# A vision block on one core: output projections in half-precision parts, second scores in full precision, a bank for each use

## The reference

```
tokens: patches of 16 x 16, real part of an rfft2, weighted, @ proj_w (192)   -> h (197 x 192)
h = h + attention1(layernorm(h))     12 heads of 16; ctx @ Wo + bo
h = h + attention2(layernorm(h))     12 heads of 64
   q, k = layernorm_head(q) * w + b, layernorm_head(k) * w + b
   o = softmax(q k^T / 8) v
   gates: softmaxes of x @ wg, wg0, wg1; the best 2 of 10 routed heads, 2 shared heads
   h + (gates * o) @ proj_w + proj_b
```

## Time and profile before

| | |
|---|---|
| median of 3 runs | 6208.34 us (6207.62 to 6211.28) |
| the profiled execution | 6208.79 us, of which the span from the first to the last instruction is 6207.0 us |
| busy share of the span | PE 94%, PE weight loads 75%, DVE 82%, ACT 80%, POOL 39% |
| TensorE's clock | full speed in nearly every slice of the span |
| transfers | 17 GB/s, about 5% of the DMA engines' time |

### The profile page before, as it was taken

One profiled execution on the slowest core, in us unless ns is written; L12 is line 12 of the kernel. 1 busy time (PEld: TensorE's weight loads), 2 busy tenths in 40 slices (PEclk: granted clock), 3 DMA queues, 4 the chain that ended last, 5 costly groups with the idle time before them and its releaser, 6 DMA issues.

```text
span 6207.0 us, 204792 instructions
## 1 busy us (share of the span) xinstructions
PE 5808.5 (94%) x63792; PEld 4640.1 (75%) x63792; DVE 5098.7 (82%) x16573; ACT 4936.7 (80%) x18945; POOL 2435.5 (39%) x2438
## 2 busy tenths in 40 slices
...
GB/s 64 16 19 16 15 19 16 15 15 19 16 15 19 16 15 15 19 16 15 19 16 15 17 17 16 15 19 16 15 19 16 15 15 19 16 15 19 16 15 5
...
## 3 DMA queue, kind: packets, MB, share of 16 engines
...
...
## 4 chain that ended last, share of the span: by engine, by line
PE 60%; DVE 27%; issue 8%; ACT 4%; DVEq 1%; SPq 0%; ACTq 0%; POOL 0%; DMA 0%; POOLq 0%
PE bank L500 54%; PE bank L684 6%; DVE nmax L1034 5%; DVE qkn L1028 4%; DVE qk L916 3%; ACT p L745 3%; DVE kl L1018 2%; DVE ql L1012 2%; DVE v L996 2%; DVE nmax L921 2%; DVE gn L1044 1%; DVE x1T L911 1%; DVE rsum L1041 1%; DVE rsum L929 0%; DVE glog L963 0%
## 5 line engine op out<-in xcount | busy, mean ns | idle before, releaser
L489 POOL TENSOR_TENSOR pq<-pq,gn 99x788 f32<-99x788 f32 x768 | 1166.3, 1519 | 2302.6 <-DVE gn L1044 2302.4
L792 ACT ACTIVATE pq<-bank,nmax 99x197 f32<-99x197 f32 x3072 | 1303.1, 444 | 300.5 <-DVE nmax L1034 300.5
L745 ACT ACTIVATE p<-bank,nmax 99x197 f32<-99x197 f32 x3072 | 1281.9, 441 | 31.2 <-DVE nmax L921 15.1
L921 DVE TENSOR_REDUCE nmax<-bank 99x2 f32<-99x394 f32 x1536 | 824.4, 565 | 320.8 <-PE bank L500 316.8
L1034 DVE TENSOR_REDUCE nmax<-bank 99x2 f32<-99x394 f32 x1536 | 837.9, 559 | 125.3 <-PE bank L500 110.1
L798 ACT ACTIVATE pT<-bank 99x394 f32<-99x394 f32 x1536 | 773.1, 512 | 152.7 <-PE bank L684 152.3
L684 PE MATMUL bank<-ident,pq 99*99 99x99 f32 (+1 forms) x6144 | 784.7, 260 | 14.8 <-ACT pq L792 3.3
L500 PE MATMUL bank<-x2T,wqkc 128*128 128x198 f16 (+1 forms) x7680 | 796.3, 249 | 1.0 <-ACT qkc L756 0.6
L684 PEld LDWEIGHTS bank<-ident,pq 99*99 99x99 f32 (+1 forms) x6144 | 647.5, 166 | 171.1 <-issue 78.4
L500 PEld LDWEIGHTS bank<-x2T,wqkc 128*128 128x128 f16 (+1 forms) x7680 | 650.0, 98 | 99.1 <-ACT qkc L756 41.4
L792 ACT ACTIVATION_READ_ACCUMULATOR pq<-bank,nmax 99x1 f32 x3072 | 687.9, 224 | 0.0
(11 more groups left out here) (149 smaller groups left out, 11877.8 us busy)
## 6 DMA issues: line engine op xcount, KB each, us to landing
xa<-in_xa SPq DMA_DIRECT2D x128, 300.1 KB
xb<-in_xb SPq DMA_DIRECT2D x128, 300.1 KB
out_tokens<-res SPq DMA_DIRECT2D x128, 74.2 KB
out_tokens<-res SPq DMA_DIRECT2D x128, 73.5 KB
...
```

The lines of the kernel that those rows point to most:

```text
L489: nc.gpsimd.tensor_tensor(pair, pair, factor, op=ALU.mult).then_inc(s_sc.up(), 1)
L745: last = nc.scalar.activation(p1[0:TC, h, c, :], psum("s1", h)[0:TC, c * T:c * T + T], ACT.Exp, bias=nmax1[:, c, h:h + 1], accum_out=sum1[ ...
L792: last = nc.scalar.activation(pq[0:TC, h % SLOTS, c, 0:T], psum("s2", h)[0:TC, c * T:c * T + T], ACT.Exp, bias=nmax2[:, h, c:c + 1], accum ...
L921: V.tensor_reduce(nmax1[:, :, h], psum("s1", h)[0:TC, 0:2 * T].rearrange("p (a b) -> p a b", a=2), op=ALU.max, axis=AX.X, negate=True).the ...
```

## The change

- `wo` and `proj` become three half-precision products each: 9 products per chunk in `wo` and 18 in `proj`, 18 and 36 MATMULs per image in place of 12 and 24. The weights are split once, ahead of the loop, scaled by 256; the copies out on DVE (`wo`, `proj`) multiply by 1/256.
- ACT's copies out (`ctx`, `o2`) now write the high part in half precision, and DVE writes the low part: new steps `cl` (3 per image) and `ol` (6 per image).
- `s2` becomes one single-precision product per head and chunk, of `qkb`. POOL makes `qkb` = `qkn` + bias, in the new step `bias` (6 per image). ACT's `rstd` and `kh` and DVE's `lo` and `kl`, 12 instructions per image on each engine, are gone.
- `ORDER` is another order on all four engines, and PE's entries name the banks: `1:s2_0@67` takes banks 6 and 7. The rings are gone.
- Two more turns at each end are written out (`LEAD`). `qk` on ACT also waits for the former image's `bias`.

```
-BANKS = {"tok": (2,), "x1T": (2,), "qk1": (0, 1), ... }
 "pe": """
+3:tok@1 0:pT_6@5 1:rstd0@0 0:pT_7@4 0:pT_8@2 1:rstd1@6 0:pT_9@5 0:pT_10@3 0:pT_11@2 0:o2_2@7 0:o2_3@3 0:o2_4@0
+0:o2_5@1 1:s2_0@67 1:s2_2@30 1:v2_0@4 3:x1T@2 0:proj@5 3:qk1_0@1 1:rstd2@4 3:qk1_1@3 3:s1_0@26 3:s1_2@01 1:s2_4@54
+1:v2_1@7 3:qk1_2@2 1:v2_2@3 1:v2_3@6 2:x2T@5 3:v1@3 3:s1_4@17 1:pT_0@6 1:rstd3@0 1:pT_1@5 2:qk0@4 2:qk1@2 1:rstd4@3
+3:s1_6@15 1:s2_6@06 2:qk2@4 1:rstd5@7 1:pT_2@2 2:qk3@1 2:gl@0 3:s1_8@34 2:qk4@7 2:qk5@0 1:pT_3@6 3:s1_10@53 1:s2_8@12
+2:ms0@7 3:ctx0@0 2:ms1 3:ctx1@6 1:s2_10@54 1:o2_0@3 2:ms2 3:ctx2@1 1:o2_1@2 1:pT_4@6 1:pT_5@0 3:wo@3
 "dve": """
+3:fold 1:var2 0:gr5 0:ol1 2:wo 1:rstd0 1:rstd1 3:tok 0:ol2 0:ol3 0:ol4 3:nx1 0:ol5 1:s2_0 1:s2_1 1:gate3 1:s2_2 1:s2_3
+1:v2_0 3:x1T 2:nx2 1:rstd2 3:qk1_0 0:proj 3:s1_0 3:s1_1 3:s1_2 1:s2_4 3:qk1_1 3:s1_3 1:v2_1 1:gr0 1:v2_2 1:s2_5 1:v2_3
+1:gr1 2:x2T 3:s1_4 3:qk1_2 1:rstd3 3:s1_5 3:ctx0 3:s1_6 1:gr2 1:s2_6 1:s2_7 1:rstd4 3:s1_7 1:rstd5 2:gl 3:s1_8 3:ctx1
+1:gr3 3:s1_9 2:gate1 3:s1_10 1:s2_8 3:s1_11 1:s2_9 2:gate2 3:ctx2 1:s2_10 1:gr4 3:cl0 3:cl1 3:cl2 1:ol0 1:s2_11
 "pool": """
+3:root1 1:bias2 3:h1b 1:h2c 2:h2b 1:sc0 1:sc1 1:bias3 2:sq0 1:sc2 2:sq1 1:bias4 1:bias5 2:sq2 2:sq3 2:sq4 1:sc3 2:sq5
+1:sc4 1:sc5 3:root2 2:bias0 2:bias1
...
+            def bias(img, t):
+                pool.wait_ge(*read_out(img, "rstd", t))
+                nc.gpsimd.tensor_tensor(qkb[:, t], qkn[:, t % QKN_SLOTS], ln_b[:].unsqueeze(2).to_broadcast([128, 2, TP]), op=ALU.add).then_inc(s_qk.up(), 1)
...
-                    for g in range(3):
-                        last = mm(o[0:TC, c * D:c * D + D], ctxT[:, g, c * TC:c * TC + TC], wo1[:, g, :], g == 0, g == 2)
+                    for n, (x, w) in enumerate(((0, 0), (1, 0), (0, 1))):
+                        for g in range(3):
+                            last = mm(o[0:TC, c * D:c * D + D], ctxT[:, g, x, c * TC:c * TC + TC], wo1[:, w, g, :], n + g == 0, n + g == 4)
...
+                pe.wait_ge(*s_qk.at(img, t + 1))
+                for c in range(2):
+                    for i in heads:
+                        r = slice(64 * (i % 2), 64 * (i % 2) + 64)
+                        last = mm(psum("s2", i)[0:TC, c * T:c * T + T], qkb[r, t, 0, c * TC:c * TC + TC], qkb[r, t, 1, 0:T])
...
-                    for t in range(6):
-                        last = mm(o[0:TC, c * D:c * D + D], oT[:, t, c * TC:c * TC + TC], wp2[:, t, :], t == 0, t == 5)
+                    for n, (x, w) in enumerate(((0, 0), (1, 0), (0, 1))):
+                        for t in range(6):
+                            last = mm(o[0:TC, c * D:c * D + D], oT[:, t, x, c * TC:c * TC + TC], wp2[:, w, t, :], n + t == 0, n + t == 7)
...
             def qk(img, t):
+                if not isinstance(img, int) or img > 0:
+                    act.wait_ge(*s_qk.at(img - 1, t + 1))
...
+            for x, dest in ((wo1_raw, wo1), (wp2_raw, wp2)):
+                link(V.tensor_scalar(dest[:, 0], x, W_SCALE, None, ALU.mult))
+                link(V.scalar_tensor_tensor(dest[:, 1], x, W_SCALE, dest[:, 0], ALU.mult, ALU.subtract))
...
+            def o_low(img, t):
+                dve.wait_ge(*s_oh.at(img, t + 1))
+                V.tensor_tensor(oT[:, t, 1, 0:T], psum("o2", t)[:, 0:T], oT[:, t, 0, 0:T], op=ALU.subtract).then_inc(free("o2", t), 1)
```

More of the change, by code:

```diff
@@ L147 @@
 """,
     "act": """
[L149 to L153, removed]
+3:x1T 1:s2_2 3:qk1_0 1:s2_3 3:qk1_1 3:s1_0 3:s1_1 3:s1_2 1:s2_4 3:qk1_2 3:s1_3 2:x2T 1:s2_5 3:v1 1:pT_0 3:s1_4 1:pT_1
```

148 lines of the change are left out of this document (52 added, 96 removed).

## The result

The changed kernel takes 5534.74 us (median of 4 runs, 5534.05 to 5535.49), the kernel before beside it 6207.98 us: ratio 0.8916, interval 0.8900 to 0.8931. I had predicted 6000 us with a range of 5870 to 6210. The direction was right, the gain more than three times what I forecast, and the time lies outside the range.

What follows compares the result with a forecast made beforehand. PE was taken as the main bound, with waits on DVE and ACT. Own work 44.5 plus waits 0.9 made 45.4 us a turn, 1.7 less over 127 turns, plus 5 us once: 6000 us, range 5870 to 6210.

Steps and rivals of the forecast that it cites:

- PE's work goes from 44.7 to 44.5: PE's own work per turn, in us: projections save 1.31, second scores add 1.1, in sum -0.2.
- Waits: PE's lost time per turn falls from 2.4 us to 0.9 us under the new order and banks.
- The one wait forecast: PE waits 0.5 to 0.6 us at `s1_0`, because DVE reads `qk1_0` out only after `rstd2`.
- Projections: On PE, `proj` falls from 3.98 to 3.07 us and `wo` from 2.00 to 1.60 us in half precision.
- Scores: On PE, each `s2` step takes 0.83 us, 0.19 more than before, with the two heads running side by side.
- Rival 4: Single precision in split rows runs one after the other on PE: `s2` 1.45 us, 6465 us in all; chance 0.09.
- The arithmetic alone is worth nearly nothing: On PE the new arithmetic saves only about 0.2 us a turn; the change stands or falls with the waits.
- The stretch in which DVE binds is gone: Between `proj` and `gl`, PE now has 15.8 us of work and DVE 12.3; before, 10.3 and 12.1.
- Engines: Busy time per turn: DVE 39.5 to 37.7 us, ACT 38.5 to 32.9, POOL 19.0 to 24.2; low parts 0.365 each.
- Rival 1: POOL's six additions a turn block DVE instructions with two SBUF inputs; 1.2 us a turn reach PE, 6150 us; chance 0.06.
- Rival 5: POOL is the late link: `s2_6` and `rstd` slip 2.5 us more than counted, 6310 us; chance 0.09.
- Rivals 2 and 3: Rival 2: saved waits come back elsewhere, 6130 us, chance 0.13. Rival 3: nothing gained, 6190 to 6220 us, chance 0.05.

Runs made afterwards that it cites:

- rstd2_first: Changed kernel with PE's `rstd2` moved ahead of `qk1_0`, nothing else: 5526.6 us, ratio 0.891 to the kernel before.
- scores_alone: Kernel before with only the new single-precision second scores and POOL's bias, old orders and bank rings: 6227.5 us, ratio 1.004 to the kernel before.
- old_order_banks: New arithmetic in the old order of all engines, each PE use naming one of 8 banks instead of rings: 6192.0 us, ratio 0.998 to before.
- before_no_lows3: Kernel before without DVE's twelve low parts a turn, all second-score products reading the high parts, PE's instructions unchanged: 6179.2 us, ratio 0.995 to before.
- new_order_new_proj: Changed kernel with the second scores put back to the old arithmetic; new projections, orders and banks kept: 6112.5 us, ratio 0.985 to the kernel before.
- old_order: Kernel before with both halves of the new arithmetic, in its old order and bank rings: 6715.3 us, ratio 1.082 to the kernel before.
- new_order_new_scores: Changed kernel with both projections back in single precision and without their low parts; new scores, orders, banks kept: 5711.7 us, ratio 0.920 to the kernel before.
- new_order_old_arith3: Changed kernel's orders and banks with all the old arithmetic, scores and projections, put back: 6179.9 us, ratio 0.996 to the kernel before.
- tuned3: Changed kernel with PE's `rstd2` ahead of `qk1_0` and `v2_1` ahead of `s1_0`: 5545.2 us, ratio 0.893 to the kernel before.
- fewer19: rstd2_first with `ms2` and `ctx2` moved ahead of `s2_10` and `o2_0` on PE, 19 division changes instead of 21: 5639.2 us, ratio 0.909 to before.

## Why the prediction was right or wrong

**The step that failed:** "PE's work goes from 44.7 to 44.5". PE's own work went from 43.9 to 41.4 us, 2.5 less where I had 0.2. I summed the arithmetic's terms and took every other step at its cost in the old order. But a step's cost depends on what stands before it. Stream fell by 0.46; 14 changes of division at 0.15 (0.12 to 0.157 measured alone) are the other 2.1, of which 0.3 lies in gaps. The old trace shows it: `o2` alone takes 3008.61 - 3007.79 = 0.82 us, and a pair of them 1.49.

```profile
3007.79 0.89 PE L500 MATMUL bank<-pT,v 128*64 128x197 f32 x8
3008.61 0.59 PE L684 MATMUL bank<-ident,pq 99*99 99x99 f32 x4
```

I used that pair only to argue that heads run side by side, and my walk of the new lists, which had the grouping before its eyes, priced each step as before.

**Waits: direction right, size short.** I had 2.4 to 0.9; measured in one way for both it is 3.2 to 0.6. Most of the gap lies on the side of before: waits shorter than the tail of the matmul ahead don't show as idle, and I allowed 0.2 us for them where there was about 1. The one wait forecast is there, at its place and size; those at `s2_4` and `wo` are not. (That rstd2_first did not end it says that DVE's reading of `qk1_0` is late for more than `rstd2` alone.)

In sum: 2.5 + 2.6 = 5.1 us a turn, against 0.2 + 1.5. The first image ends 22 us earlier, where I had 5 us more; why is open, and it is 3% of the gain.

**Projections: right, a little high.** 2.97 and 1.49 us. I had taken 0.12 us for each step's start from `v1`, which is followed by `s1`, another division. That is the price of a change, and both projections now stand between steps of their own division.

**Scores: right.** 0.84 us against 0.83 where `s2` stands alone, 0.755 in the one pair; heads side by side, their first matmuls 7 ns apart. Rival 4 is false.

**"The arithmetic alone is worth nearly nothing": right** (scores_alone, old_order_banks). **"The stretch in which DVE binds is gone": wrong as a cause in the old order** (before_no_lows3), right, as far as new_order_new_proj separates it from ACT's work, as a condition of the new one: with DVE at 42 us the order doesn't hold.

**Engines.** DVE 38.1 us (37.7 forecast), ACT 33.8 (33), POOL 23.3 (24). The low parts take 0.360 and 0.359 (0.365):

```profile
L1019 DVE TENSOR_TENSOR oT<-bank,oT 128x197 f16<-128x197 f32 x768 | 266.0, 360 | 42.5 <-ACT oT L782 42.4
...
L1015 DVE TENSOR_TENSOR ctxT<-bank,ctxT 128x197 f16<-128x197 f32 x384 | 127.1, 359 | 90.4 <-ACT ctxT L739 90.4
```

**Rivals.** Rival 1 (POOL blocks DVE) is false, though its mechanism exists. With POOL's six additions in the old order (old_order) the mean of `gn` rose from 232 to 326 ns; in the changed kernel it is 166, with 951 at most. In new_order_new_scores another DVE instruction with two SBUF inputs, `xs`, takes 1905 ns in place of 965, begun while POOL's `sc` is 0.4 us into its 1.5, and PE's waits stay at 0.6 us. How often the two meet depends on the order and the arithmetic. In new_order_old_arith3, where DVE is full, `xs` and `gpair` take 1.6 us a turn more than before; what of it reaches PE is open. Rival 5: PE waited 6.8 us in the whole run for POOL's `qkb`. Rivals 2 and 3 did not come in the changed kernel; of rival 2, that saved waits come back elsewhere, tuned3 and fewer19 are examples.

**The range.** Every case in it moved the time by waits or by the price of one new step; none let PE's own work fall through the order. (Its own range, 5880 to 6090, holds the bounds of the waits alone; with those it names for projections and scores added it would begin at 5810. The result is below that too.)
